# Last step of the batch loop: another bank for the third shared product group, another order of the tile list, the weight rests and the late weight loads

## What is computed

```
h = attention(x)                       # 16 heads of 16
h = concat([cls_tok, h], axis=1)       # 513 rows a batch
h = h + state_scan(layernorm(h))       # linear recurrence over the rows
h = h + ffn(layernorm(h))

ffn(u): out = silu(u @ Wg_s.T) * (u @ Wu_s.T) @ Wd_s.T         # shared expert, 512 inner features
        scores, idx = top_k(sigmoid(u @ Wr.T + rb), 2)         # router over 8 experts
        out += cw[e] * silu(u @ Wg[e].T) * (u @ Wu[e].T) @ Wd[e].T   # for the two chosen experts
```

## Time and profile before

| | us |
|---|---|
| median of 3 runs | 1162.68 |
| range of the runs | 1161.87 to 1164.88 |
| profiled execution | 1163.81 |
| its span | 1161.9 |
| TensorE busy in the span | 1116.7 (96%) |
| last step and head of the expert stage, TensorE | from about 760.5 to 797.1 |

### The profile page before, as it was taken

One profiled execution on the slowest core, in us unless ns is written; L12 is line 12 of the kernel. 1 busy time (PEld: TensorE's weight loads), 2 busy tenths in 40 slices (PEclk: granted clock), 3 DMA queues, 4 the chain that ended last, 5 costly groups with the idle time before them and its releaser, 6 DMA issues.

```text
span 1161.9 us, 22261 instructions
## 1 busy us (share of the span) xinstructions
PE 1116.7 (96%) x6090; PEld 718.5 (62%) x6091; DVE 916.8 (79%) x1571; ACT 584.2 (50%) x973; POOL 394.3 (34%) x508
## 2 busy tenths in 40 slices
PE   9999999999999999989999999969999999999996
PEld 5654333333333333477777787757888888888885
DVE  4788888888888887678888888777777777777774
ACT  4445777777777777631233222432444444444442
POOL 2002621011111101214345443353555555554553
PEclk9998999999999999989999999999999999999998
DMA  7887333332333322041244541122333333333332
GB/s 232 273 273 259 92 89 88 93 99 81 95 85 90 103 72 87 1 164 42 68 109 109 100 98 39 38 47 78 55 55 54 51 56 52 51 53 54 54 55 32
DMA packets 109714, 105.37 MB, mean 91 GB/s; under 512 B 42464, under 2 KB 97904, under 8 KB 109648
## 3 DMA queue, kind: packets, MB, share of 16 engines
q1 hardware_dynamic: 92704, 85.38, 26.2%
q0 software_dynamic: 16960, 19.38, 10.5%
HBM read 64.88 MB, written 39.68 MB: 90 GB/s over the span
## 4 chain that ended last, share of the span: by engine, by line
PE 73%; DVE 10%; issue 3%; POOL 3%; ACT 1%; another core or an unknown queue 0%; DMA 0%; POOLq 0%; DVEq 0%; ACTq 0%
PE mix_pairs L73 20%; PE pv L688 11%; PE by_key L675 10%; PE by_query L666 9%; PE mix_made L1874 9%; PE mix_turn L1861 3%; POOL kept_table L1130 3%; PE mix_made L1282 2%; PE mix_made L1270 2%; PE by_query L709 2%; PE mix_turn L1841 1%; PE mix_pairs L1308 1%; PE mix_made L1253 1%; DVE mix_stats L1462 1%; DVE k_mix_u L1472 1%
## 5 line engine op out<-in xcount | busy, mean ns | idle before, releaser
L762 DVE TENSOR_REDUCE k_neg_max<-by_query 128x2 f32<-128x1024 f32 x240 | 282.8, 1220 | 48.4 <-PE by_query L666 45.2
L823 ACT ACTIVATE k_wu_e<-by_key 128x512 f32<-128x512 f32 x512 | 270.1, 600 | 64.9 <-PE by_key L675 64.8
L675 PE MATMUL by_key<-k_wg_e 99*128 99x512 bf16 x512 | 175.1, 384 | 2.8 <-PEq L147 2.4
L1818 POOL DMA_INDIRECT out_rows<-x_y,k_slot x72 | 114.0, 1583 | 156.1 <-PE mix_turn L1841 104.6
L666 PE MATMUL by_query<-k_wg_e 96*128 96x512 bf16 x480 | 144.7, 382 | 0.0
L1918 ACT ACTIVATE x_gate<-mix_pairs 128x512 f32<-128x512 f32 x72 | 43.0, 597 | 196.8 <-PE mix_pairs L73 196.8
L688 PE MATMUL pv<-k_wu_e,k_wd_e 128*17 128x512 f32 x1024 | 134.5, 598 | 0.3 <-ACT k_wu_e L823 0.3
L73 PE MATMUL mix_pairs<-w_short,x_T 128*128 x288 | 120.8, 419 | 2.2 <-issue 2.2
L1874 PEld LDWEIGHTS mix_made<-x_wd,x_acts_T 128*128 128x128 f32 x864 | 111.2, 188 | 7.4 <-ACT x_acts_T L1941 0.9
L73 PE MATMUL mix_pairs<-w_short,x_rest 128*128 x288 | 113.9, 396 | 0.0
L1874 PE MATMUL mix_made<-x_wd,x_acts_T 128*128 128x256 f32 x864 | 112.6, 279 | 0.7 <-ACT x_acts_T L1941 0.7
(11 more groups left out here) (251 smaller groups left out, 1960.8 us busy)
## 6 DMA issues: line engine op xcount, KB each, us to landing
k_wg_e<-kept_qk SPq DMA_DIRECT2D x384, 64.0 KB, 2.3
kept_qk<-k_qk_parts SPq DMA_DIRECT2D x32, 384.0 KB, 3.4
kept_v<-k_v_ones SPq DMA_DIRECT2D x8, 544.0 KB, 5.3
k_wd_e<-kept_v SPq DMA_DIRECT2D x32, 136.0 KB, 2.7
k_wu_e<-in_xT SPq DMA_DIRECT2D x8, 512.0 KB, 4.6
kept_heads<-k_wd_e SPq DMA_DIRECT2D x8, 512.0 KB, 3.0
k_heads_in<-kept_heads SPq DMA_DIRECT2D x8, 512.0 KB
k_wg_e<-in_wg_e SPq DMA_DIRECT2D x8, 512.0 KB, 4.7
```

Source lines behind the costliest of these rows:

```text
L675: pe.matmul(by_key[:, key_bank(job), :], k_rows[0:SROWS, g, h, kt * P:(kt + 1) * P], q_rows[0:SROWS, g, h, :], start=True, stop=True).then ...
L762: dve.tensor_reduce(neg_max[:, g % 2, 2 * n:2 * n + 2], by_query[:, bank:bank + 2, :], AX.X, ALU.max, negate=True).then_inc(query_read, 1)
L823: act.activation(probs[:, key_tile(j) // 2 * G + j // 2 % G, j % 2, :], by_key[:, key_bank(job), :], ACT.Exp, scale=float(HD) ** -0.5).the ...
L1818: pool.indirect_dma_start(out=dram["out"], in_=y[:, r % 2, :], in_offset=None, compute_op=ALU.add, out_offset=bass.IndirectOffsetOnAxis(ap ...
```

## The change

On TensorE group 2 of the last step now goes to the `made` banks and waits for `h2_done` of all batches; group 3 goes to `pairs[:, 0]` and waits for the consumer of group 0. Two fillers are added behind the last router product and four between the groups and `shared_down`, the latter waiting for the consumer of group 2. At the head of the expert stage 15 fillers stand ahead of the first transpose and 10 behind it; the waits for the weights come behind those; the gate product of tile 0 asks for 14 rests, then the second transpose follows, and the up product asks for all 16. On VectorE `list_passed` moves from behind group 1 to behind group 2, and `list_skipped` from behind group 2 to behind group 3; cut 6 moves behind it, and the cuts' order becomes 6, 8, then 10, 12, then 14, 7, 9, 11, and 13, 15 in the expert stage. On SyncE `load_late` moves behind the four slot loads and waits there for the first two gathered tiles.

```diff
--- before.py
+++ after.py
@@ -1022,6 +1022,12 @@
 
         PROJECT_BEHIND, STATE_BEHIND = (4, 5, 6, 8), (8, 9, 10, 12)
 
+        def up_banks(j, m):
+
+            if j == B - 1 and m >= 2:
+                return made[:, :, :] if m == 2 else pairs[:, 0, :, :]
+            return pairs[:, m % 2, :, :]
+
         def batches(eng, step):
             for b in range(B + 1):
                 step(b, b % 2, b > 0, b < B, b < B - 1)
@@ -1070,13 +1076,16 @@
                     sp.wait_ge(mem["lists_made"], 1)
                     needed = sp.value_load(mem["full_i"][0:1, 0:1], min_val=16 * (1 + TT * (B - 2)),
                                            max_val=16 * (1 + TT * B))
-                    load_late()
 
                     sp.wait_ge(slots_out[0], 16 * (1 + TT * B))
                     sp.wait_ge(slots_out[1], needed)
                     sp.wait_ge(mem["lists_made"], 2)
                     for r in range(FIRST_X):
                         load_slot(sp, mem, dram, slot_tile(sp, mem, 0, r), r)
+
+                    for r in range(2):
+                        sp.wait_ge(mem["x_gathered"][r], 16)
+                    load_late()
                 if prev and not this:
                     store_out(b, par)
 
@@ -1156,7 +1165,7 @@
             def silu(j, m):
                 act.wait_ge(ev["gate_made"], FC * j + m + 1)
                 act.wait_ge(ev["down_made"], 2 * j)
-                act.activation(gate[:, m, :], pairs[:, m % 2, 0, :], ACT.Silu).then_inc(ev["gate_done"], 1)
+                act.activation(gate[:, m, :], up_banks(j, m)[:, 0, :], ACT.Silu).then_inc(ev["gate_done"], 1)
 
             def copy_turned(to, b, turned, copied):
                 act.wait_ge(ev[turned], b + 1)
@@ -1291,11 +1300,15 @@
                     pe.wait_ge(ev["acc_done"], 2 * j)
                     pe.wait_ge(ev["w_s_cut"], 2)
                     pe.wait_ge(ev["u2_cut"], j + 1)
+                elif j == B - 1 and m == 2:
+                    pe.wait_ge(ev["h2_done"], 2 * B)
+                elif j == B - 1 and m == 3:
+                    pe.wait_ge(ev["act_done"], FC * j + 1)
                 elif m >= 2:
                     pe.wait_ge(ev["act_done"], FC * j + m - 1)
                 for n in kinds:
                     for c in range(DC):
-                        mm = split_products(pe, pairs[:, m % 2, n, :],
+                        mm = split_products(pe, up_banks(j, m)[:, n, :],
                                             (w_s_short[:, n, c, m * P:(m + 1) * P], w_s_rest[:, n, c, m * P:(m + 1) * P]),
                                             (u2_short[:, c, :], u2_rest[:, c, :]), start=(c == 0), stop=(c == DC - 1))
                 if kinds[-1] == 1:
@@ -1350,6 +1363,9 @@
                     turn_heads(b + 1)
                     project_out(b + 1)
                 if prev:
+                    if not this:
+                        pe.wait_ge(ev["act_done"], FC * b - 1)
+                        mem["keep_awake"](pe, 4)
                     shared_down(b - 1, 0)
                     shared_down(b - 1, 1)
                 if this:
@@ -1376,6 +1392,8 @@
                             mm = pe.matmul(turn[:, 0, t * E:(t + 1) * E], u2_T[:, c, t * P:(t + 1) * P],
                                            mem["wr_T"][:, c, :], start=(c == 0), stop=(c == DC - 1))
                     mm.then_inc(ev["logits_made"], 1)
+                    if not nxt:
+                        mem["keep_awake"](pe, 2)
                     if prev:
                         shared_up(b, 0, (0, 1) if nxt else (0,))
 
@@ -1441,7 +1459,7 @@
             def shared_act(j, m):
                 dve.wait_ge(ev["gate_done"], FC * j + m + 1)
                 dve.wait_ge(ev["down_made"], 2 * j)
-                dve.tensor_tensor(gate[:, m, :], gate[:, m, :], pairs[:, m % 2, 1, :], ALU.mult).then_inc(ev["act_done"], 1)
+                dve.tensor_tensor(gate[:, m, :], gate[:, m, :], up_banks(j, m)[:, 1, :], ALU.mult).then_inc(ev["act_done"], 1)
 
             def shared_add(j, par, half):
                 dve.wait_ge(ev["down_made"], 2 * j + half + 1)
@@ -1533,13 +1551,9 @@
                         place(b - 1, 1 - par)
                     shared_act(b - 1, 0)
                     if not this:
-
                         dve.wait_ge(ev["counts_read"], b)
                         count_tiles(dve, cls_link, mem, flat_backs)
-                        cut_weights(dve, mem, 6)
                     shared_act(b - 1, 1)
-                    if not this:
-                        list_passed(dve, cls_link, mem, flat_backs)
                 if 1 <= b <= EARLY:
                     cut_weights(dve, mem, b - 1)
                 if this and prev:
@@ -1548,10 +1562,11 @@
                 if prev:
                     shared_act(b - 1, 2)
                     if not this:
-                        list_skipped(dve, cls_link, mem, flat_backs)
+                        list_passed(dve, cls_link, mem, flat_backs)
                     shared_act(b - 1, 3)
                     if not this:
-                        for n in (7, 8, 9):
+                        list_skipped(dve, cls_link, mem, flat_backs)
+                        for n in (6, 8):
                             cut_weights(dve, mem, n)
                 if this:
                     dve.wait_ge(ev["ud_done"], 2 * b + 2)
@@ -1573,11 +1588,12 @@
                 if prev:
                     shared_add(b - 1, 1 - par, 0)
                     if not this:
-                        for n in (10, 11, 12):
+                        for n in (10, 12):
                             cut_weights(dve, mem, n)
                     shared_add(b - 1, 1 - par, 1)
                     if not this:
-                        for n in (13, 14):
+
+                        for n in (14, 7, 9, 11):
                             cut_weights(dve, mem, n)
                 if this and not nxt:
                     cut_weights(dve, mem, 5)
@@ -1875,19 +1891,21 @@
                                    start=(n == 0 and m == 0), stop=(n == 2 and m == FC - 1))
             mm.then_inc(ev["down_made"], 1)
 
+        pe.wait_ge(mem["lists_made"], 2)
+        first = expert(pe, 0)
+        mem["keep_awake"](pe, 15)
+        turn_x(0, 0)
+        mem["keep_awake"](pe, 10)
         for e in range(3):
             pe.wait_ge(mem["expert_in"][e], 16 * 3)
         pe.wait_ge(mem["experts_in"], 16 * 3 * (E - 3))
-        pe.wait_ge(mem["lists_made"], 2)
-        first = expert(pe, 0)
-        mem["keep_awake"](pe, 9)
-        for t in range(2):
-            turn_x(0, t)
-            mem["keep_awake"](pe, 4)
+        pe.wait_ge(mem["acc_done"], 2 * B)
+
+        pe.wait_ge(mem["ev_cut"]["rest_made"], 2 * E - 2)
+        up(0, 0, 0, first)
+        turn_x(0, 1)
         pe.wait_ge(mem["ev_cut"]["rest_made"], 2 * E)
-        pe.wait_ge(mem["acc_done"], 2 * B)
-        for which in range(2):
-            up(0, 0, which, first)
+        up(0, 0, 1, first)
 
         def body(i, last):
             following = expert(pe, R * i + 1)
@@ -2005,7 +2023,8 @@
                 weigh(i, r)
 
         copy_x(0, 0)
-        cut_weights(dve, mem, 2 * E - 1)
+        for n in (2 * E - 3, 2 * E - 1):
+            cut_weights(dve, mem, n)
         copy_x(1, 1)
         cut_down(0, 0)
         act(0, 0)
```

## The result

The changed kernel takes 1168.63 us (median of 5 runs, 1166.23 to 1171.22), the kernel before in the same comparison 1162.68 us (1161.14 to 1164.88). The ratio is 1.0051, interval [1.0029, 1.0073]: about 6 us slower where 6 us faster was forecast. All ratios and intervals here use the fast executions, which leaves out one execution of e10, at 2870.21 us. The profiled execution of the change took 1166.23 us. It is the quickest of the five, 2.42 us above the profiled execution of the kernel before, where the medians differ by 5.95.

A forecast was written before the change was run, and what follows sets the result against it. The prediction took VectorE's list of cuts, begun late because group 3 was late, as the bound at the step's end. 1163.81 less 5.9 gave 1157.9 us, and 1156.8 for the median, 1.1 lower; range 1154.8 to 1164.8.

The forecast's parts named there:

- Groups 2 and 3: TensorE, last step: without the old waits group 3's last result comes at about 773.1 instead of 775.02, 1.9 us earlier.
- The prompt count: Behind group 3: its count comes without delay, fourth Silu at 773.2, consumer done at 774.6, 7.3 us earlier.
- the order of the rests: VectorE's cuts: 15.6 us with no idle time, rests complete at 790.2; gate product needs two cuts less, 787.9.
- The late load: SyncE, behind the second gather: issued near 784.9, in at 790.8 after 5.9 us, setting the gate product's start.
- the forecast's base: Head of the expert stage: up product at 792.6 instead of 798.5, 5.9 us earlier, taken from the profiled 1163.81 us.
- VectorE behind group 3: From group 3's consumer to the last rest: 10 cuts, list, adds and copy, 15.6 us, complete at 790.2.
- first rival: Count stays late: consumer ends at 780.0, rests complete 797.3, up product only 0.8 us earlier, 1161.9 us; chance 0.23.
- second rival: Late load lands late (793) and TensorE's clock falls, slowing the first products: 1159 to 1161.6 us; chance 0.15.
- third rival: Groups really last until their Silus, consumer stays at 781.9: 1164.1 to 1166.7 us, middle 1164.8; chance 0.17.

The follow-up runs named there:

- e10: Changed kernel with the list back ahead of group 3 and `load_late()` between slot loads and gathers, rests' order new; ratio 1.0022.
- e2: Kernel before with only the bank change and TensorE's new waits for groups 2 and 3; ratio 1.0006.
- e3: Changed kernel with `load_late()` back where it was, ahead of the slot loads; ratio 1.0054.
- e5: Kernel before with the last batch's 8 table scatters held until the last group of shared products is counted; ratio 1.0033.
- e6: Changed kernel with the last batch's 8 table scatters held until the last group of shared products is counted; ratio 1.0071.
- e8: e7 with the last batch's 8 table scatters held until the last group of shared products is counted; ratio 1.0051.
- e13: Kernel before with the last batch's 8 table scatters moved behind the first two gathers, first down matrix waiting for them; ratio 1.0039.
- e14: e7 with the last batch's 8 table scatters moved behind the first two gathers; ratio 1.0027.
- e7: Changed kernel with VectorE's order of list and rests (gate product waiting for 16) and the late load's place both as before; ratio 1.0009.
- e15: e7 with the new place of the tile list on VectorE; ratio 1.0003.
- e18: Changed kernel, unchanged, profiled once more; this execution took 1162.98 us.
- e9: Changed kernel with the list back ahead of group 3 and the late load back, rests' order new; ratio 1.0038.
- e11: Changed kernel with both VectorE orders and the late load back, without the 4 fillers ahead of `shared_down` and their wait; ratio 1.0002.
- e16: e7 with the gate product waiting for 15 of the 16 rests; ratio 1.0020.
- e4: Changed kernel with VectorE's old order of list and rests, gate product behind 16 rests, late load still behind the gathers; ratio 1.0032.

## Why the prediction was wrong

**Groups 2 and 3** end 2.15 us earlier (774.45 shifted is 772.87, against 775.02): 1.9 were forecast. Right.

Three steps failed: the prompt count, the order of the rests taken as free, and the time at which the late load goes out.

**The prompt count** is the step that failed first. I chose it because I put the lateness down to TensorE standing still between groups and to SyncE's wait on the same count. The changed kernel, e2 and e3 have neither gap nor, in the first, SyncE's wait there, and are as late. What the lateness of groups 2 and 3 needs is GpSimd's table scatters beside them: group 2 is over 1 us late in 11 of 14 executions that have them there, and in none of the 6 from which an edit took them away. The choice overlooked this third thing that is particular to the last step. One batch earlier GpSimd's last scatter stands well ahead of the prompt pair in the earlier trace rows:

```profile
730.46 0.97 POOL L1130 DMA_INDIRECT kept_table<-k_pay,k_slot_i  x1 [0.30 <-issue]
```

But scatters alone don't make a count late. Group 0 is prompt in all 20 executions, though they run beside it in 19. Group 1 is prompt in e5, e6 and e8 and 2.1 us late in e13 and e14, with the same 8 scatters beside it. And the lateness varies between executions of one kernel (6.6 and 0.04 us for group 3 of the changed one). By what path a scatter holds the count back, and what decides, stays open.

That makes the forecast's base wrong too. Its 5.9 us were in the main the difference between a late and a prompt execution, which no edit of the change brings about: e7 and e15, which keep the old load and the old rests, reach D 32.9 and 32.6 when prompt. The kernel before has no prompt profile here, but its runs beside e5 to e8 spread from 1156.7 to 1163.5 us, as wide as the forecast gain. That its quick runs are the prompt ones is argued, not shown.

**VectorE behind group 3** was summed as one chain of 15.6 us, with the order of the rests free. The sum itself came out: in e18 the rests are complete 16.1 us behind the consumer of group 3 (774.83 to 790.93) and no add waits; in the late execution it is 17.0 us (782.39 to 799.37) with two waits of 0.98 and 0.49 us ahead of the adds, where the first rival had 17.3. What failed is that the order is free. With late counts VectorE waits for a half of `shared_down` whatever it does (3.05 us in e9, 1.85 in e11), so cuts ahead of that add are covered and cuts behind the last add are not, and the change moved two of them behind the last add. The rows of tile 0 are copied 14.8 us behind the consumer of group 3 in e9 and 13.2 in e11. The cost is about 3.4 us by the medians of these two, which differ also in e11's missing fillers, but e11 and e7, which has them, can't be told apart. With prompt counts the order costs nothing that shows: 13.8 us in e18, 13.9 in e7. The wait that the order bought, fewer rests asked for, is worth about 1.1 us (e7: rows copied at 788.2, last rest made at 789.4), and e16, which asks for 15, doesn't show it.

**The late load** is in at most 6.4 us behind its issue (792.10 to 798.52, and 787.65 to 794.05 in e18; 5.9 forecast). Its place fails: even with nearly prompt counts it goes out at 787.65, not 784.9, since GpSimd's last scatters end at 781.7 and gathers begin at 781.97, 1.2 us later than I took, and need 5.7 us from the first gather's issue to the load's, where I had 4.1. That is my second rival. Its mechanism holds and its price was too low: it took the gate product to 793 and the whole time to 1159 to 1161.6 us, and e18 has 794.05 and 1162.98. TensorE's granted clock is 0.50 in the stretch behind its 3.98 us of idle time. The Trainium skill says in "TensorE: Matmul & The Clock Gate", section "HAM oscillation — how this bites in real kernels", that a wait for a DMA brings the slow clock and that the burst behind the wait pays for it; the trace of e18 agrees. In a late execution the load costs less, for the rows are nearly as late: 798.5 against 797.1 here.

**Why the costs don't add.** Rests and load each hold the same start. Load new alone is e4, 1.0032; rests and list new alone is e3, 1.0054; both is the change, 1.0051; neither is e7, 1.0009. The profiles show which came last: in e4 the load (gate product 796.39, rows copied at 790.8), in e3 the rows (copied at 799.4, gate product 799.66). Whichever is last is paid, so undoing one of them gave little or nothing back.

**First and third rivals.** The first profile comes out nearly as the first rival: consumer of group 3 ends at 782.4, shifted 780.8 (780.0 forecast), rests complete at 797.8 shifted (797.3), late load at 796.9 shifted (796.2), up product at 800.16, shifted 798.6 (797.7). Its 1161.9 us is still 6.7 under the median. By its own sign, a consumer later than 780.5, the third rival would have been taken as true. But its reading, that the products themselves last until the Silu, is refuted: e5 runs them at the same pace with prompt Silus. That its price, 1164.8, was nearer to the median than mine is luck. The range ended there, 3.8 us short of the median.

## What to carry to other kernels

An unexplained delay in a profile is not free to be assumed away by an edit that doesn't touch its cause; first profile the same kernel twice, since the delay, and with it the gain, may belong to one execution. Where an engine waits anyway, work ahead of the wait is free and the same work behind it is paid: count the pieces of work on each side of every wait, not only their sum. A load moved behind a chain of small transfers inherits that chain's worst case, and its price is hidden only as long as something else is as late.

## Unexpected from the hardware

While GpSimd issues indirect scatters (about 1.28 us apart), the other engines can see TensorE's counts late, measured from the modelled end of the matmul that raises them: ScalarE by up to 10.6 us (e9, e10), SyncE by up to 8.0 (e16, 774.55 to 782.50), VectorE by up to 1.9 (e18, 764.49 to 766.43). A small part of a Silu's lateness can be the Silu ahead of it: in e9 the last two start at 780.61 and 781.10, while SyncE saw the last count by 780.73. For groups 2 and 3 without scatters beside them it was 0.04 us, and once 0.7. Scatters whose last issue ended at 795.24 had to be waited for until about 800 (e13; 792.80 and 797.6 in e14), so a buffer under them is held some 5 us longer than GpSimd's timeline suggests.
